# A Perceiver block on one Trainium2 core: two projections and the norm between them in one block, a reciprocal moved, the last squares read from PSUM

## What is computed

```python
x = x + xattn(layernorm(x), ctx_2048, ...)      # 16 heads, int8-like rounding of q, k, v and probabilities, @ Wp + bp
x = x + attn(layernorm(x), ...)                 # causal, rope on q and k, softmax, @ Wo + bo
x = x + ffn(layernorm(x), ...)                  # fp4 weights; y = (silu(gate) * up) @ down;  y / sqrt(mean(y*y) + 1e-6)
```

## Time and profile before

| | us |
|---|---|
| median of 3 runs (lowest, highest) | 2726.31 (2723.64, 2727.68) |
| the profiled execution: its time | 2726.34 |
| the profiled execution: its span, first to last instruction | 2724.6 |
| TensorE busy in the span | 2518.8 (92%) |
| VectorE, ScalarE, GpSimd busy | 2071.9, 1142.0, 868.9 |

### The profile page before, as it was taken

How to read it: one execution, slowest core, us unless ns; L and a number is a source line. 1 busy time by engine, 2 the same in 40 slices (tenths; PEclk the granted TensorE clock), 3 DMA queues, 4 the chain that set the end, 5 groups by cost and what they waited for, 6 DMA issues and landing times. The chain is left out here.

```text
span 2724.6 us, 42839 instructions
## 1 busy us (share of the span) xinstructions
PE 2518.8 (92%) x16296; PEld 1282.2 (47%) x16296; DVE 2071.9 (76%) x2977; ACT 1142.0 (42%) x1096; POOL 868.9 (32%) x429
## 2 busy tenths in 40 slices
PE   6999999999999999999888888888868999999998
PEld 3444444444444444444354545545554458444443
DVE  7798877877787778777799999999965344766664
ACT  4222222222222222222499999999972124311100
POOL 0323321332133213321465756656530550111100
PEclk9999999999999999999899999999989995999999
DMA  6234443344334433443688888888872232000000
GB/s 256 60 92 110 123 122 102 92 123 123 94 98 123 123 97 96 123 123 93 162 196 210 190 197 200 203 209 189 198 210 96 107 67 45 1 16 16 1 4 31
DMA packets 557346, 321.56 MB, mean 118 GB/s; under 512 B 401968, under 2 KB 533296, under 8 KB 552368
## 3 DMA queue, kind: packets, MB, share of 16 engines
q1 hardware_dynamic: 557232, 319.91, 45.5%
HBM read 149.95 MB, written 69.21 MB: 80 GB/s over the span
## 5 line engine op out<-in xcount | busy, mean ns | idle before, releaser
L1287 DVE TENSOR_SCALAR_CACHE_REDUCE at_sc<-at_score 128x1024 f32<-128x1024 f32 x512 | 601.7, 1220 | 12.0 <-PE at_score L1162 6.0
L1386 ACT ACTIVATE at_sc<-at_sc,at_bias,at_qs 128x4096 uint16<-128x4096 f32 x128 | 484.9, 3792 | 1.1 <-DVE at_bias L1299 1.1
L655 PE MATMUL kv_vacc<-wt_stage,kv_xthi 128*128 128x512 f16 x1024 | 388.1, 379 | 1.3 <-PEq L279 1.3
L655 PE MATMUL kv_vacc<-kv_wlo,kv_xthi 128*128 128x512 f16 x1024 | 388.1, 379 | 0.0
L655 PE MATMUL kv_vacc<-wt_stage,kv_xtlo 128*128 128x512 f16 x1024 | 388.1, 379 | 0.0
L663 PE MATMUL kv_kacc<-kv_wk,q_t 128*128 128x512 f16 x1536 | 347.2, 379 | 0.0
L734 ACT ACTIVATE q_t<-q_t 128x512 f16<-128x512 f32 x128 | 77.1, 626 | 489.3 <-POOL q_t L937 319.5
L935 POOL TENSOR_TENSOR q_t<-kv_rows 128x512 f32<-128x512 f32 x32 | 41.5, 1295 | 692.2 <-DMA kv_rows<-in_ctx 610.0
L740 ACT ACTIVATE o<-wt_stage 128x1024 f16<-128x1024 f32 x64 | 67.6, 1057 | 407.2 <-DVE wt_stage L826 407.2
L663 PEld LDWEIGHTS kv_kacc<-kv_wk,q_t 128*128 128x128 f16 x1536 | 150.3, 98 | 181.2
L663 PE MATMUL kv_kacc<-kv_wk,kv_xthi 128*128 128x512 f16 x768 | 228.4, 379 | 0.9 <-DVE kv_xtlo L512 0.9
(11 more groups left out here) (228 smaller groups left out, 4243.7 us busy)
## 6 DMA issues: line engine op xcount, KB each, us to landing
kv_rows<-in_ctx SPq DMA_DIRECT2D x64, 512.0 KB, 7.0
values<-wt_stage SPq DMA_DIRECT2D x32, 1024.0 KB, 6.4
keys_turned<-o SPq DMA_DIRECT2D x32, 1024.0 KB, 5.1
wt_stage<-values SPq DMA_DIRECT2D x16, 2048.0 KB, 8.7
wt_stage<-keys_turned SPq DMA_DIRECT2D x32, 512.0 KB, 5.1
x<-keys_turned SPq DMA_DIRECT2D x31, 512.0 KB, 5.2
x<-in_x SPq DMA_DIRECT2D x2, 2048.0 KB, 8.8
kv_wk<-in_wq SPq DMA_DIRECT2D x2, 2048.0 KB, 13.4
```

The lines of the kernel that those rows point to most:

```text
L655: last = nc.tensor.matmul(v_acc[2 * s + c][:], a[s][:, k, :], b[:, c, k, :], start=(k == 0 and q == 0), stop=(k == KD - 1 and q == 2))
L1287: nc.vector.tensor_scalar(sc[n % 2][:, c * SC:(c + 1) * SC], score[pos % 2][:], 1.0, None, ALU.mult, ALU.max, accum_out=part_max[n % 2][:, ...
L1386: nc.scalar.activation(prob[n % 2][e], sc[n % 2][:, e * EC:(e + 1) * EC], ACT.Exp, bias=bias[n % 2][:], scale=qs_pair[j][:, t:t + 1], accu ...
```

## The change

1. `start_loads`, `project` "pp" and `project` "ps" become one block, `project_twice`. SP issues the six small loads at its start, then the panels. TensorE's order is by tiles: four units of transposes, the first group of products, the other four units, then groups in the order (tile, half) = (1,0), (0,1), (1,1), (2,0), (2,1), then the normalised tiles 0 and 1 are transposed, then (3,0), (3,1), then tile 2, and after two groups of the next projection tile 3. VectorE normalises each tile as soon as both halves are taken (`normalise`), with a square root for each tile on ScalarE. GpSimd adds the bias row by tiles.
2. The halves of `o` get a place of their own in `space`, and panel 2 (the first half of Wq) leaves the ring for a place in `space` (`panels.keep`), so neither waits for what is read.
3. In `attend_causal` the reciprocal of group g is taken as soon as the exponentials of group g are done (`invert`), after `outputs(g-1)`; `outputs` only multiplies.
4. At the end of the program the squares of the first halves are summed early, from `y`; the squares of the second half are taken by ScalarE from PSUM with the scale in the instruction, beside VectorE's `take(1, t)`, which now comes after the mean of its tile is made.

```diff
+def project_twice(chip, panels, o, o_parts, x, x_parts, ident32, row, rows, addend, out, beside):
...
+    ORDER = [(0, 0), (1, 0), (0, 1), (1, 1), (2, 0), (2, 1), (3, 0), (3, 1)]
...
+            sp.dma_start(*row).then_inc(row_loaded, 16)
+            for pair in rows:
+                sp.dma_start(*pair).then_inc(rows_loaded, 16)
+            while panels.next_load < len(panels.sources):
+                panels.load(sp, panels.next_load)
...
+            def first_products(at):
+                t, n = ORDER[at]
+                pe.wait_ge(o_lo_ready, 2 * t + 2)
+                pe.wait_ge(panels.lo_ready, n + 1)
+                if t >= 2:
+                    pe.wait_ge(panels.taken, ORDER.index((t - 2, n)) + 1)
+                products(acc_of(t, n), o_hi, o_lo, t, n)
...
+            def second_products(n, t):
+                if n == 0:
+                    pe.wait_ge(x_lo_ready, 2 * t + 2)
+                    pe.wait_ge(panels.taken, T + t + 1)
+                elif n >= 2:
+                    pe.wait_ge(panels.taken, 2 * T + T * (n - 2) + t + 1)
+                products((bank if n % 2 else acc)[t], xt_hi, xt_lo, t, n + 2)
...
+            panels.high(act, 0)
+            for n in range(4):
+                high_o(n)
+            panels.high(act, 1)
+            for n in range(4, 8):
+                high_o(n)
+            panels.high(act, 2)
+            root(0)
+            root(1)
+            root(2)
+            for n in range(4):
+                high_x(n)
+            root(3)
+            for n in range(4, 8):
+                high_x(n)
+            for m in range(3, COUNT + 3):
+                panels.high(act, m)
...
+            def normalise(t):
+                for n in range(2):
+                    dve.wait_ge(panels.taken, ORDER.index((t, n)) + 1)
+                    nc.vector.bn_stats(stats[:, t, n, :], x[:, t, n * HALF:(n + 1) * HALF]).then_inc(stat_step, 1)
...
+                rsqrt_steps(nc, dve, norm_step, 5 * t, root_ready, t + 1, var, root, tmp, rstd)
...
+            for t in range(T):
+                nc.gpsimd.tensor_tensor(x[:, t, :], x[:, t, :], row[0], ALU.add).then_inc(row_added, 1)
+            beside(pool)
...
+            def invert(g):
+                dve.wait_ge(exps_done, HG * (g + 1))
+                nc.vector.reciprocal(inv[g % 2][:], total[g % 2][:]).then_inc(inv_ready, 1)
+
             def outputs(g):
                 t, c = groups[g]
+                dve.wait_ge(inv_ready, g + 1)
                 dve.wait_ge(summed, g + 1)
-                nc.vector.reciprocal(inv[g % 2][:], total[g % 2][:]).then_inc(inv_ready, 1)
-                dve.wait_ge(inv_ready, g + 1)
...
                 if g >= 1:
                     outputs(g - 1)
+                invert(g)
...
             def finish(t):
-                dve.wait_ge(squared, t + 1)
...
+                dve.wait_ge(squared, T + t + 1)
+                total, var, root, tmp, rstd, first_half = (small[:, k, t:t + 1] for k in range(6))
+                nc.vector.tensor_scalar(var, total, 1.0 / D, first_half, ALU.mult, ALU.add).then_inc(mean_ready, 1)
+                take(1, t)
...
             for t in range(T):
-                take(1, t)
-                if t:
-                    finish(t - 1)
-            finish(T - 1)
+                finish(t)
...
-                nc.scalar.activation(sq, y[:, t, :], ACT.Square, accum_out=small[:, 0, t:t + 1]).then_inc(squared, 1)
...
+            for t in range(T):
+                act.wait_ge(summed, UP_SUMMED + T * (2 * NB - 1) + t + 1)
+                act.wait_ge(squared, T + t - 1)
+                nc.scalar.activation(sq[t % 2], halves[1][t][:], ACT.Square, scale=DOWN_OUT,
+                                     accum_out=small[:, 0, t:t + 1]).then_inc(squared, 1)
```

More of the change, by code:

```diff
@@ L239, in __init__, with keep @@
         self.next_load = 0
+    def keep(self, n, parts):
+        self.to[n], self.in_ring[n] = parts, False
     def place(self, chip, ctx):
@@ L1729, in project_and_feed_forward @@
         hid = [chip.sb(ctx, f"ff_hid{j}", [P, T * P], F32) for j in range(2)]
[L1730 removed]
+        small = chip.sb(ctx, "ff_small", [P, 6, T], F32)
         stats = chip.sb(ctx, "ff_stats", [P, T, 2, nc.vector.BN_STATS_DIM], F32)
@@ L1736, in project_and_feed_forward @@
                           (room["hi"], pair0[0]), (room["lo"], pair0[1]))
-        sq = weights.sign[:, 0:2, :].rearrange("p a n -> p (a n)").bitcast(F32)
+        sq = [sig[j][:] for j in range(2)]
         acc = [[chip.ps(ctx, f"ff_acc{j}{g}", [P, T * P], F32) for g in range(2)] for j in range(2)]
@@ L1986, in _ @@
             for t in range(T):
-                act.wait_ge(taken, T + t + 1)
-                if t:
-                    act.wait_ge(squared, t)
-                nc.scalar.activation(sq, y[:, t, :], ACT.Square, accum_out=small[:, 0, t:t + 1]).then_inc(squared, 1)
+                act.wait_ge(taken, t + 1)
+                if t >= 2:
+                    act.wait_ge(squared, t - 1)
+                nc.scalar.activation(sq[t % 2], y[:, t, 0:HALF], ACT.Square,
+                                     accum_out=small[:, 5, t:t + 1]).then_inc(squared, 1)
+            for t in range(T):
+                act.wait_ge(summed, UP_SUMMED + T * (2 * NB - 1) + t + 1)
+                act.wait_ge(squared, T + t - 1)
+                nc.scalar.activation(sq[t % 2], halves[1][t][:], ACT.Square, scale=DOWN_OUT,
+                                     accum_out=small[:, 0, t:t + 1]).then_inc(squared, 1)
                 act.wait_ge(mean_ready, t + 1)
@@ L2082, in build @@
             panels = panels2
-            panels.place(chip, c)
             WORDS_AT = 8 * D + NSC * HALF // 2
@@ L2095, in build @@
             y_v, y_q, y_k = rows_at(0), rows_at(9 * D), rows_at(13 * D)
+            first_keys = space[:, 0:4 * D].bitcast(F16).rearrange("p (q k n) -> p q k n", q=2, n=HALF)
+            panels.keep(2, (first_keys[:, 0], first_keys[:, 1]))
+            panels.place(chip, c)
             q_t = space[:, 4 * D:8 * D].rearrange("p (k n) -> p k n", n=T * P)
```

177 lines of the change are left out of this document (162 added, 15 removed).

## The result

The changed kernel takes 2707.43 us in the median of 4 runs (2706.27 to 2709.0), beside 2726.99 us (2723.64 to 2728.91, 4 runs) for the kernel before on the same chip. The ratio is 0.993, with a 95% interval of 0.9918 to 0.9942. The forecast was 2708. The profiled execution's span is 2707.2 us, where the kernel before had 2724.6.

A forecast was written before the change was run, and what follows sets the result against it. TensorE, busy 92% of the span, was taken as the bound, with gains only between long products, in causal attention and at the end: 12.2 + 4.2 + 2.2 = 18.6 us off 2726.3 gives 2707.7, forecast 2708, range 2701 to 2715.

The forecast's parts named there:

- Part 1: Start of the projections' block: it starts 0.52 us after GpSimd ends, a gain of 3.98 us.
- Part 2: First group of products: starts 9.4 us after the block's start, net gain 1.0 us, less 1.6 for the clock.
- Part 3: Norm between the projections: no TensorE wait remains, 3.6 us of transposes replace 12.4 us without products; gain 8.8 us.
- the clock term: First group of products: 2.5 us lost to the lower clock after a rest, 1.6 more than before.
- Part 4: Causal attention: early reciprocal cuts the group period from 4.73 to 4.43 us, 14 groups at 0.30; gain 4.2 us.
- Part 5: Program end: last scaling starts 2.5 us after the last matmul, where it was 4.7; gain 2.2 us.
- The first, the clock that rises: Rival in causal attention: clock rises once gaps go, period 2.7 us a group, 22 us more gained, 2686; chance 0.07.
- The norm's chain: Rival between projections: `normalise` or panel 2 over 6 us late, TensorE waits, about 8 us given back, 2716; chance 0.08.
- the exponentials: Rival in causal attention: another wait takes the reciprocal's place, part 4 gives 0, 2712; chance 0.07.
- the lower clock in the first projection: Rival: clock stays low there, each group of 24 costs 5.2 us more, 2747 with all eight cold; chance 0.03.
- rival 5: Whole change: gains nothing since the blocks' border is paid in another place, 2725; chance 0.03.

The follow-up runs named there:

- projections only: The kernel before with only one block for both projections and panel 2 out of the ring; 2713.67 us, ratio 0.9953.
- panel 2 in the ring: The changed kernel without the call of `keep`, so the third weight panel's halves take their turn in the ring; 2710.99 us, ratio 0.9941.
- sums first: The changed kernel with causal attention's output products of the group before placed ahead of the transposes of the exponentials; 2710.70 us, ratio 0.9938.
- the reciprocal by itself: The kernel before with only the reciprocal taken as soon as the exponentials are done; 2722.52 us, ratio 0.9985.
- the end's part alone: The kernel before with only the last squares taken from PSUM; 2724.01 us, ratio 0.9990.
- the fillers outside the causal stage: The changed kernel with unread matmuls: 30 behind the new block's first 16 transposes, 19 and 7 around the last transposes ahead of the feed-forward; 2703.82 us.
- 3 fillers a group: The changed kernel with 12 unread matmuls ahead of causal attention's first transposes and 3 ahead of each later group's; 2697.29 us, ratio 0.9894.
- fillers at the start: The changed kernel with 12 unread matmuls ahead of the first group's transposes in causal attention; 2701.25 us, ratio 0.9905.
- causal stage covered: The changed kernel with unread matmuls ahead of causal attention's transposes: 12 in the first and seventh groups, 18 in the tenth, 3 in others; 2689.15 us.
- all fillers: The changed kernel with unread matmuls in causal attention (12, 12, 18, 3 ahead of others) and in three stretches outside (30, 19, 7); 2683.16 us.
- fillers in long waits: The kernel with both filler sets, but in causal attention only 12, 14 and 20 ahead of the first, seventh and tenth groups' transposes; 2684.61 us.
- loads apart: The changed kernel with the six small loads again in a block of their own ahead of the projections; 2713.31 us, ratio 0.9954.

## Why the prediction was right, by its own steps

**Part 1, the block start: right.** Forecast 0.52 us behind GpSimd and 3.98 us gained; measured 0.53 and 3.97. The loads in a block of their own give 3.86 of it back, so SP's block was the cause. The quarter by quarter additions took 17.14 us where one of four tiles took 11.86, but the first takes waited for none of them.

**Part 2, the first group: sizes off.** Products began 9.33 us after the block's start (forecast 9.4). The clock loss was mis-sized: I took 2.5 us and it was 6.73 - 5.18 = 1.55. That it is the clock, and nothing else, the fillers in this wait show, with 5.18 us for the group. The lower level lasted 3.1 us into the group, and half of that time is what it costs. But the term isn't a constant of the kernel: in the profiled executions of the seven kernels that start alike (the changed one, projections only, panel 2 in the ring, sums first and the three with fillers in causal attention alone) the group took 6.64 to 7.68 us, a loss of 1.5 to 2.5. My value was the upper end.

**Part 3, the norm between the projections: right.** No wait of TensorE, 3.5 us of transposes between groups (forecast 3.6). The smallest margin was the one named, panel 3's low half: done at 2104.76, wanted at 2106.3. Panel 2's own room was needed, as the 2.12 us without it show. From GpSimd's last multiplication to the last product it was 195.9 us before and 182.6 after: 13.3 gained, 12.2 forecast, the difference being the clock term.

**Part 4, the reciprocal: right in direction, its period mis-sized.** The step that failed is "TensorE is then the bound at 4.73 - 0.30 = 4.43 us". The 0.30 us are idle time of the weight loads (PEld), which overlap with the matmuls. The matmuls themselves were busy for 3.99 of 4.00 us there, so the 0.30 could not all be gained. Of it 0.22 remain whoever releases TensorE; they follow the scores, as the experiment with the sums first showed. The period is 4.65, and the flat part gains only 0.08 a group, about 1 us in all.

The stage gained 3.6 us nonetheless (4.2 forecast), because of two things outside the flat part: one that I had put at nothing, and one that I had not looked at. ScalarE's half of the panel held TensorE for 0.81 us and no longer does, and the last period, with no scores in it, went from 4.72 to 3.26 us. TensorE's waits for exponentials at these places, before (timeline):

```profile
2264.92 1.12 PE L1519 MATMUL ca_turn<-ident,ca_s 128*128 128x128 f32 x4 [0.81 <-ACT ca_s L1582]
...
2308.93 1.12 PE L1519 MATMUL ca_turn<-ident,ca_s 128*128 128x128 f32 x4 [2.01 <-ACT ca_s L1582]
```

and after, where the first is gone:

```profile
2292.69 1.12 PE L1745 MATMUL ca_turn<-ident,ca_s 128*128 128x128 f32 x4 [0.54 <-ACT ca_s L1812]
```

Two errors nearly cancelled here, which is luck. That the sum belongs to this edit the reciprocal by itself shows, with 3.52 us.

**Part 5, the end: right.** From the last matmul (2700.46) to the last scaling (2702.89) 2.43 us, forecast 2.5. The square from PSUM with its read-out took 0.70, as estimated.

**What the sum left out.** Behind the causal stage 1.36 us were given back: *output* is 404.72, where the end's part alone gives 403.36. The 32 transposes took 6.20 instead of 5.72, and the last 8 took 1.98 on the path where 0.73 had stood. The kernel with panel 2 in the ring has the same code there and shows 403.36, and the kernel with the projections alone has the code of the kernel before and shows 407.16 against 405.67. So it is no cost of that code. It goes with the clock: in the changed kernel the clock rose 5.2 us after the stage's first transpose, in the kernel before and with panel 2 in the ring 3.6 us after it. What decides that from one kernel to the next stays open. With the fillers outside the causal stage this stretch is 3.85 us shorter than in the changed kernel, and its 32 transposes still take 5.72 us there, where the kernel with 3 fillers a group, at the full clock, has 4.49; so more of the clock is left in it.

**The sum.** Beside the forecast's 18.6 us the projections gave 1.1 more, the causal stage 0.6 less and the end 0.1 more, and the stretch behind the causal stage took 1.4 back: 17.8. The two profiled executions differ by 17.3 us (2726.34 and 2709.0, the slowest of the four), the medians by 19.6. That the median lies 0.6 us from the forecast is therefore luck in part; the terms missed by up to 1.4 us in both directions, and the executions of one kernel spread over 2.7 and 5.3 us.

**The rivals.** The first, the clock that rises, did not come: 0.53 in the stage. The Trainium skill, page "TensorE: Matmul & The Clock Gate", section "What's actually happening", says that activity releases the throttle. The changed kernel doesn't bear it out in busy time, 4.00 of 4.00 us at 0.50; the kernel with 3 fillers a group may, since there the clock came back some 17 us after its fall. The price was fair, though: with the long waits covered the stage runs at 1.00 and the period is 2.93 us on average (four of them in 2239.09 - 2227.38 = 11.71, without fillers between), near the 2.7 estimated for that rival. I had the condition wrong: ahead of the falls in the stage stood whole waits, and the clock did not come back although TensorE no longer waits for exponentials in an ordinary group. What keeps it low through windows that are busy for 4.00 of 4.00 us no run here shows. The norm's chain, the exponentials and the lower clock in the first projection (rivals 2, 3 and 4) did not come either: no idle, no release by a reciprocal, and 1.00 from the second group on. Nor did rival 5.

## What to carry to other kernels

A block that only issues loads holds every engine for its length (3.9 us here); put the issues into the next block's queue, and let its first users wait by semaphores. When the trace names a releaser for a short wait, ask what else stands in that gap, and whether the row is one of weight loads or of matmuls, before you count all of it as a gain: here 0.22 of 0.30 us stayed. Where a stage is at TensorE's lower clock, look for the waits ahead of the fall, not only at the busy share: with three of them filled the causal stage went from 77.81 to 57.64 us, which is more than any edit of this change gave (12.8).

## What the runs showed of the hardware

- TensorE stayed at 1.2 GHz for 70 us, windows of 4.00 of 4.00 us busy among them, and at 2.4 GHz for 52 us with 48.19 busy, on the same operations with 46 fillers among them. What it did before the falls: idle for 1.73, 1.76, 2.63 and 2.85 us. Behind the 1.26 us ahead of the first scores the clock fell 2.0 us later in two kernels (fillers at the start, causal stage covered) and stayed at 1.00 in three with the same code there (3 a group, all fillers, fillers in long waits). Idle stretches of 0.67 us, one in every second group, were followed by no fall.
- Going from the scores of 64 rows to an operation of 128 rows costs TensorE a little: at 1.2 GHz the first matmul behind the scores starts 0.35 us after the last of them, whichever operation it is, where the scores stand 0.21 us apart. That is the idle 0.22 us of the weight loads. At 2.4 GHz the two figures are 0.20 and 0.11 us (fillers in long waits).
- VectorE's low half of a panel and GpSimd's additions don't run side by side; one waits for the other to end. A low half takes 4.42 us by itself and an addition 2.34. In the changed kernel an addition that began 0.62 us into a low half took 6.02 us, and the next low half, begun 0.15 us into an addition, took 6.48: in either case the rest of the other's time and then its own. The second addition runs from 2038.27, the third from 2040.57 (timeline). 2040.57 - 2038.42 + 4.43 = 6.58, which is near the 6.48. The 1.18 us in the kernel with the loads apart are the same, since its addition ended 1.33 us after the low half began. VectorE's four low halves of `o` ran beside an addition and kept their 0.62 us each, so it isn't so for every operation. The Trainium skill, page "SBUF — State Buffer", section "SBUF: two separate sides", says that the two engines share a port pair as an exclusive lock, taken by a VectorE operation with two SBUF inputs, and that the loser fully blocks. The traces agree, with 6.02 and 6.48 us: the low half of a panel has two such inputs, those of `o` read one operand from PSUM. The lengthened low half of this kernel (timeline):

```profile
2038.42 6.48 DVE L267 SCALAR_TENSOR_TENSOR wt_ring<-wt_stage,wt_ring 128x4096 f16<-128x4096 f32 x1
```
